# A vision tower whose patch convolution is split: two groups of images first, the other fourteen in strips between the first groups' chains

## Chip, cores, metric

The kernel runs on one NeuronCore of a Trainium2 chip. The metric is the device time of one execution in microseconds, lower is better, given as the median of several runs.

## What is computed

64 images of 2 x 104 x 104 are joined with four copies of themselves shifted by 4 pixels (zero filled), normalised per image over all ten channels, weighted, and turned into 13 x 13 tokens of 128 features by an 8 x 8 patch convolution. A class token is put ahead, and a graph layer, an attention layer and a gated mixture of eight experts follow.

```python
lu, ru, ld, rd = _shifts(x)
concat = jnp.concatenate((x, lu, ru, ld, rd), axis=1)
mean = jnp.mean(concat, axis=(1, 2, 3), keepdims=True)
var = jnp.var(concat, axis=(1, 2, 3), keepdims=True)
normed = (concat - mean) * jax.lax.rsqrt(var + EPS)
normed = normed * gamma[None] + beta[None]
y = jax.lax.conv_general_dilated(normed, W, window_strides=(PATCH, PATCH), padding='VALID', ...)
...
h = jnp.concatenate([broadcast cls_tok, h], axis=1)
h = h + gcn(_layernorm(h))                  # edges, relu, four 128x128 maps
hx = _layernorm(h); causal attention with l2-normalised q, k; y = o @ Wo
gate = softmax(y @ gate_W + gate_b)
out = h + sum over 8 experts of gate * (gelu(y @ W1 + b1) @ W2 + b2)
```

## The kernel before, in words

The order of the work is written out by hand for five engines that meet only at semaphores: SP (loads and most stores), POOL, ACT, PE and DVE. Within an engine everything runs in the order of the program, so whatever waits holds up all that is queued behind it. Features lie on the 128 partitions, tokens along the free dimension.

**Convolution.** Row `p` of 13 rows of cells has 13 cells x 64 images = 832 columns. For each of 5 shifts DVE multiplies the loaded cells by gamma (L1006) into one of two sets of five `xg` tiles, and PE multiplies the product by `conv_w` (L650, in `conv`), five shifts summed in PSUM; `conv_ps` alternates between two PSUM pairs, so that ACT can copy row `p-1` out (L451, `tokens_out`) while PE works on row `p`. The convolution runs on cells that are not normalised; beside it ACT squares each row of cells (L446), DVE adds up the squares (L991) and POOL adds up the cells (L373). `prepare(p)` puts small pieces between the rows: one-hot tables (L946) for the graph matrix, the products of gamma and beta with the weights (L615), the graph maps and the split of weights into f16 pairs (L966 to L980).

**Image statistics.** After row 13 DVE reduces the sums to one column per image (L1019 to L1027), PE averages over partitions (L659), and DVE and ACT make a scale and a shift for all 64 images in `img` (L1030 to L1039).

**The chain of a group.** Four images (680 tokens) form a group, 16 groups. `early` corrects the tokens of a group with `img` (fix0 to fix3, L1066 and L1069), takes the layer norm (mean, dev, sq, var, three Newton steps of a reciprocal root on DVE at L1052 to L1059, cast back over partitions by PE at L692, xn) and applies the graph (edges, relu0 to relu3 at L485). `graph` adds the four maps (L664), the residual h2 and the second norm; `queries_keys` makes q and k and their norms. Then `attention` and the experts (`ffn`, 32 slots: L869 in, L564/L569 gelu, L1213 low part, L886 out, L1225 weighing). In the loop of groups each step of `early(g + 2)`, `graph(g + 1)` and `queries_keys(g + 1)` has a slot inside `ffn(g)` (tables EARLY_SLOTS and others). Groups 0 and 1 have no experts of earlier groups around them: their chains run after the convolution, one step after the other, before the first attention.

**Weights.** w1 and w2 (4 MB) are loaded late in the convolution and right after it; POOL splits them into f16 high and low parts (L387, L389, 32 instructions) while the chains of groups 0 and 1 run, and PE waits for all of them before the first experts. POOL also issues the accumulating stores of the expert outputs.

## Time and profile before

| | us |
|---|---|
| median of 3 runs (1611.28 to 1613.82) | 1611.56 |
| the profiled execution, its own time | 1615.64 |
| span of the profile | 1613.8 |
| PE busy / DVE busy / ACT busy / POOL busy | 1495.1 / 1211.3 / 1099.5 / 227.3 |
| mean granted TensorE clock (1 is 2.4 GHz) | 0.963 |

The profile is one execution. Busy is the time in which an engine worked on an instruction, and the idle time before an instruction is put down to whatever released it. A PE that is busy at the lower clock does half as much. The page cuts the span into 40 slices of 40.3 us:

```profile
PE   5993589999999999999999999999999999999998
...
DVE  7994358787868778787878787887878787877665
...
POOL 5376101010110101010101101010101010110101
PEclk8995589999999999999999999999999999999979
```

### The profile page before, as it was taken

What the parts mean: (1) busy time and instruction counts of PE and PEld (TensorE: products, weight loads), DVE (VectorE), ACT (ScalarE), POOL (GpSimd) and SP (SyncE); (2) the same over time, 40 slices, a digit from 0 to 9 for tenths busy, and PEclk for the clock granted to TensorE, in tenths of its full rate; (3) what the DMA queues carried; (4) which work ended last, traced back from release to release, by engine and by line L of the source; (5) the groups of instructions that cost most, each with busy time, mean ns of one, the idle gap of its engine ahead of it and who ended that gap; (6) DMA issues with size and microseconds to landing.
All of it is one profiled execution on the core that took longest, in us unless ns stands there. A gap on an engine that the chain in (4) does not pass through costs nothing.

```text
span 1613.8 us, 31251 instructions
## 1 busy us (share of the span) xinstructions
PE 1495.1 (93%) x10837; PEld 1020.8 (63%) x10837; DVE 1211.3 (75%) x2510; ACT 1099.5 (68%) x1879; POOL 227.3 (14%) x213
## 2 busy tenths in 40 slices
PE   5993589999999999999999999999999999999998
PEld 3551356666666666666666666666666666667665
DVE  7994358787868778787878787887878787877665
ACT  2321157777777777777777777777777777777766
POOL 5376101010110101010101101010101010110101
PEclk8995589999999999999999999999999999999979
DMA  5312004243333333241423333233324242433323
GB/s 189 116 65 79 9 5 110 36 104 43 97 51 95 42 89 52 59 80 26 112 35 104 43 95 47 92 43 91 49 45 94 33 109 38 104 43 97 53 88 53
DMA packets 33714, 113.48 MB, mean 70 GB/s; under 512 B 5008, under 2 KB 5008, under 8 KB 31120
## 3 DMA queue, kind: packets, MB, share of 16 engines
q0 software_dynamic: 18432, 44.57, 20.5%
q1 hardware_dynamic: 14960, 67.71, 11.4%
q10 hardware_dynamic: 288, 0.77, 0.1%
q8 instruction: 18, 0.29, 0.1%
q14 instruction: 16, 0.13, 0.0%
HBM read 62.56 MB, written 50.48 MB: 70 GB/s over the span
## 4 chain that ended last, share of the span: by engine, by line
PE 59%; DVE 28%; issue 7%; ACT 4%; DVEq 1%; DMA 1%; POOL 0%; POOLq 0%; ACTq 0%
PE pair L886 20%; PE pair L869 17%; PE pair L664 7%; DVE area L1213 5%; PE pair L650 4%; DVE area L1135 3%; DVE root_t L1055 2%; PE pair L783 2%; DVE area L1142 2%; DVE area L1225 2%; PE pair L692 1%; PE pair L676 1%; PE pair L817 1%; PE pair L739 1%; PE pair L810 1%
## 5 line engine op out<-in xcount | busy, mean ns | idle before, releaser
L564 ACT ACTIVATE area<-pair,pack_b_sb 128x680 f32<-128x680 f32 x512 | 422.8, 828 | 220.4 <-PE pair L869 217.8
L1213 DVE TENSOR_TENSOR area<-area 128x680 f16<-128x680 f32 x512 | 441.1, 864 | 149.3 <-ACT area L569 143.8
L886 PE MATMUL pair<-area,ws 128*128 128x340 f16 x3072 | 529.8, 307 | 12.9 <-DVE area L1225 11.8
L869 PE MATMUL pair<-area,ws 128*128 128x340 f16 x3072 | 527.1, 308 | 0.0
L886 PEld LDWEIGHTS pair<-area,ws 128*128 128x128 f16 x3072 | 284.3, 98 | 168.8 <-DVE area L1225 44.1
L869 PEld LDWEIGHTS pair<-area,ws 128*128 128x128 f16 x3072 | 297.8, 98 | 143.7 <-issue 0.2
L569 ACT ACTIVATE area<-pair,pack_b_sb 128x680 f16<-128x680 f32 x384 | 316.4, 824 | 0.0
L401 POOL DMA_DIRECT2D tower_out<-area x128 | 109.7, 857 | 1266.8 <-DVE area L1225 1205.3
L1225 DVE SCALAR_TENSOR_TENSOR area<-pair,pack_b_sb,area 128x340 f32<-128x340 f32 x256 | 134.0, 565 | 28.9 <-PE pair L886 19.9
L528 ACT ACTIVATE area<-pair,nbias,root 85x85 f32<-85x85 f32 (+1 forms) x256 | 112.4, 464 | 22.4 <-DVE nbias L1123 22.4
L650 PE MATMUL pair<-area,pack_a_sb 128*128 128x512 f32 (+1 forms) x260 | 97.1, 533 | 18.4 <-DVE area L1006 18.4
L650 PEld LDWEIGHTS pair<-area,pack_a_sb 128*128 128x128 f32 x260 | 50.7, 198 | 62.5 <-issue 42.9
L664 PE MATMUL pair<-area,gcn_m 128*128 128x340 f32 x256 | 83.4, 461 | 0.0
L1120 DVE TENSOR_REDUCE mx<-pair 85x4 f32<-85x340 f32 x64 | 41.0, 680 | 55.8 <-PE pair L787 55.8
L1006 DVE TENSOR_TENSOR area<-area,pack_a_sb 128x832 f32<-128x832 f32 x65 | 75.1, 1218 | 7.7 <-DMA pack_a_sb<-pack_a 6.3
L1211 DVE CAST area<-area 128x680 f16<-128x680 f32 x128 | 65.6, 513 | 19.7 <-ACT area L564 14.4
L451 ACT ACTIVATE ht<-pair 128x832 f32<-128x832 f32 x13 | 22.5, 1730 | 75.9 <-PE pair L650 75.9
L485 ACT ACTIVATE area<-pair,pack_b_sb 128x680 f32<-128x680 f32 x64 | 59.2, 935 | 20.2 <-PE pair L664 19.7
L373 POOL TENSOR_TENSOR area<-area 128x896 f32<-128x896 f32 x13 | 57.0, 4383 | 39.0 <-DMA area<-cells 38.0
L664 PEld LDWEIGHTS pair<-area,gcn_m 128*128 128x128 f32 x256 | 47.4, 195 | 18.0 <-issue 1.4
L798 PE MATMUL pair<-ident,area 85*85 85x85 f32 x384 | 45.4, 256 | 13.4 <-DVE area L1135 13.4
L1135 DVE TENSOR_SCALAR area<-area,rs 85x85 f32<-85x85 f32 (+1 forms) x256 | 55.7, 278 | 2.3
(182 smaller groups left out, 1640.7 us busy)
## 6 DMA issues: line engine op xcount, KB each, us to landing
tower_out<-area POOLq DMA_DIRECT2D x128, 340.0 KB, 4.6
area<-gate_scratch SPq DMA_DIRECT2D x16, 1360.0 KB, 9.9
area<-gate_scratch SPq DMA_DIRECT2D x16, 1020.0 KB, 7.1
area<-cells SPq DMA_DIRECT2D x14, 448.0 KB, 3.7
tower_out<-ht SPq DMA_DIRECT2D x16, 340.0 KB, 2.3
area<-gate_scratch SPq DMA_DIRECT2D x16, 340.0 KB, 4.4
area<-cells SPq DMA_DIRECT2D x13, 416.0 KB, 4.3
area<-w SPq DMA_DIRECT2D x1, 2048.0 KB, 10.1
```

Of the source, the lines that this page charges most:

```text
L401: pool.dma_start(out[:, g * T:(g + 1) * T], tmp[e % 2], accum_op=ALU.add).then_inc(out_done, 16)
L528: nc.scalar.activation(probs[:, b * SCORE + o0:b * SCORE + o0 + w], score_ps_at(b)[:, h, c * QC:c * QC + w], ACT.Exp, bias=nbias[:, n:n + ...
L564: nc.scalar.activation(two(hid[slot % NHID]), halves(hid_ps[slot % 2]), ACT.Gelu_apprx_tanh, bias=col(COL_B1 + slot)).then_inc(hid_ready, 1)
L569: nc.scalar.activation(two(hh[slot % NPART]), halves(hid_ps[slot % 2]), ACT.Gelu_apprx_tanh, bias=col(COL_B1 + slot)).then_inc(hhi_act, 1)
L650: last = mm(flat(conv_ps(p))[:, a:b], conv_w[:, s * D:(s + 1) * D], xg[p % 2][s][:, a:b], start=(s == 0), stop=(s == SHIFTS - 1))
L664: last = mm(fr_ps[:, j, 0:TH], lhs, rhs[:, j, :], start=start, stop=stop)
L869: last = mm(hid_ps[slot % 2][:, j, 0:TH], lhs[:, w], rhs[:, j * TH:(j + 1) * TH], start=(i == 0), stop=(i == 2))
L886: last = mm(eo_ps[:, j, 0:TH], lhs[:, w], rhs[:, j * TH:(j + 1) * TH], start=(m % CH == 0 and i == 0), stop=(m % CH == CH - 1 and i == 2))
L1006: v.tensor_tensor(xg[p % 2][s].rearrange("p (j b) -> p j b", b=B), src[:, c0 * B:(c0 + NP) * B].rearrange("p (j b) -> p j b", b=B), gv, AL ...
L1135: last = v.tensor_scalar(p, p, rs[:, n:n + 1], None, ALU.mult)
L1213: v.tensor_tensor(hl[slot % NPART], hid[slot % NHID], hh[slot % NPART], ALU.subtract).then_inc(hlo_ready, 1)
L1225: v.scalar_tensor_tensor(tmp[e % 2][:, j * TH:(j + 1) * TH], eo_ps[:, j, 0:TH], b2_s[:, e:e + 1], gbc[:, e * T + j * TH:e * T + (j + 1) * ...
```

## The change

The images are cut in two parts. The 8 images of groups 0 and 1 (`BA`) are loaded whole (`first0`, `first1`), multiplied and convolved at once for the full 13 x 13 cells (`gammas_first`, `conv_first`), and get their own sums (16 accumulating activations on ACT, borders on DVE) and their own factors. The other 56 images (`BZ`) are convolved as before in 13 rows of 728 columns, now counted as 65 points (row x shift). `xg` is a ring of six single products. The four tables FIRST_0, GRAPH_0, QK_0 and FIRST_1 name, for each step of the chains of groups 0 and 1, the point behind which it stands, on PE, ACT and DVE alike; PE_PREP, DVE_PREP and ACT_PREP do so for the preparations. The first two groups take their first mean with f32 matmuls straight from the tokens, so POOL has no part in it. The factors of the 56 images are finished between attention(0) and the first experts (15 small DVE instructions, no square root on ACT). A row of the strips has one PSUM pair (`eo_ps`, 7 and 6 cells in its two halves); its two halves are copied out by two ACT instructions, and the next row waits for them. The weights come expert by expert through four buffers: POOL splits experts 0 to 3 after its sums, and 4 to 7 ahead of its stores of group 0; PE waits for each expert's split inside the experts, in every group. `part_h`, `part_l` and `k_wide` have moved to other addresses.

```diff
+FIRST_0 = {"tail": 4, "fix0": 5, "fix1": 5, "fix2": 6, "fix3": 6, "mean": 7, "dev": 9, "sq": 10, "var": 11, "root0": 13,
+           "root1": 13, "root2": 13, "cast": 14, "xn": 16, "xn_lo": 16, "edges": 18, "relu0": 19, "relu1": 19,
+           "relu2": 19, "relu3": 19}
+GRAPH_0 = {"plain": 22, 0: 22, 1: 23, 2: 23, 3: 24, "h2": 26, "mean2": 27, "dev2": 29, "sq2": 30, "var2": 31,
+           "roots2": 33, "cast": 34, "hx": 36, "hx_lo": 36}
+QK_0 = {"q": 38, "sums_q": 40, "k": 40, "sums_k": 42, "root0": 44, "root1": 44, "root2": 44, "wide": 45,
+        "cast": 46, "kn": 48}
...
+BA = 2 * NB
+BZ = B - BA
+CHUNKS = ((0, 4), (4, 7), (7, 10), (10, NP))
+CELLS = ((0, 7), (7, NP))
+XG = 6
+PE_PREP = {7: 2, 10: 3, 14: 4, 19: 5}
+DVE_PREP = {4: 1, 6: 2, 9: 3, 17: 5}
+ACT_PREP = {3: 3, 11: 4, 15: 5, 20: 6}
...
-R1, R0 = 4, 4
+R1, R0 = 4, 3
...
+        M1, M0 = NG1 * NG1 * BA, NP * NP * BA
+        all1, all0 = take(M1, ws), take(M0, ws)
+        ag = [take(M0, ws) for _ in range(2)]
+        edge_a = take(2 * 4 * NG1 * BA, ws)
+        junk = [take(NG1 * NG1, ws) for _ in range(BA)]
...
+        row0 = [take(N0) for _ in range(R0)]
+        xg = [take(N0) for _ in range(XG)]
...
+            def weights(e):
+                if e >= 2:
+                    sp.wait_ge(wlo_done, 2 * (e - 1))
+                for k, w in enumerate((w1, w2)):
+                    sp.dma_start(staged[e][k], w[:, e * FF:(e + 1) * FF]).then_inc(w_in[e], 16)
+
+            sp.dma_start(all0, first0).then_inc(all0_in, 16)
+            sp.dma_start(all1, first1).then_inc(all1_in, 16)
+            sp.dma_start(packs["pack_b"][:, :], pack_b).then_inc(pack_b_in, 16)
             load0(0)
...
-            tokens_lo(0)
-
-            for i in range(2 * E):
-                part, first = (i * FF // STAGE, i * FF % STAGE) if i < E else (2, (i - E) * FF)
-                pool.wait_ge(w_in[part], 16)
-                hi, lo = (w1h, w1l) if i < E else (w2h, w2l)
-                w, src = slice((i % E) * FF, (i % E + 1) * FF), staged[part][:, first:first + FF]
-                pool.tensor_copy(hi[:, w], src).then_inc(whi_done, 1)
-                pool.wait_ge(whi_done, i + 1)
-                pool.tensor_tensor(lo[:, w], src, hi[:, w], ALU.subtract).then_inc(wlo_done, 1)
-
-            tokens_lo(1)
+            def split(e):
+                pool.wait_ge(w_in[e], 32)
+                for k, (hi, lo) in enumerate(((w1h, w1l), (w2h, w2l))):
+                    w, src = slice(e * FF, (e + 1) * FF), staged[e][k]
+                    pool.tensor_copy(hi[:, w], src).then_inc(whi_done, 1)
+                    pool.wait_ge(whi_done, 2 * e + k + 1)
+                    pool.tensor_tensor(lo[:, w], src, hi[:, w], ALU.subtract).then_inc(wlo_done, 1)
+
+            pool.wait_ge(part_step[0], 3)
+            pool.wait_ge(conv_a, len(CHUNKS))
+            for e in range(4):
+                split(e)
...
+                    if g == 0 and e + 4 < E:
+                        split(e + 4)
...
+            def sums_first():
+
+                act.wait_ge(all1_in, 16)
+                for n, func in enumerate((ACT.Copy, ACT.Square)):
+                    for b in range(BA):
+                        if n:
+                            act.wait_ge(sums_a, b + 1)
+                        nc.scalar.activation(junk[b], all1.rearrange("p (c b) -> p b c", b=BA)[:, b, :], func,
+                                             accum_out=stats[0][:, n * BA + b:n * BA + b + 1]).then_inc(sums_a, 1)
...
+            def tokens_out(p, j):
+                act.wait_ge(conv_done, 2 * p + j + 1)
+                t0, t1 = (1 + p * NP + c for c in CELLS[j])
+                dst = ht[:, BA * TOK:].rearrange("p (b t) -> p t b", t=TOK)[:, t0:t1, :]
+                nc.scalar.activation(dst, cells_ps(j).rearrange("p (j b) -> p j b", b=BZ), ACT.Copy).then_inc(tok_done, 1)
...
+            sums_first()
+            act.wait_ge(pack_b_in, 16)
+            nc.scalar.activation(ht[:, :].rearrange("p (b t) -> p t b", t=TOK)[:, 0, :],
+                                 col(COL_CLS).broadcast_to([128, B]), ACT.Copy).then_inc(tok_a, 1)
+            for c in range(len(CHUNKS)):
+                tokens_first(c)
+            squares(0)
+            prep_evac(2)
+            for n in range(POINTS):
+                p, shift = divmod(n, SHIFTS)
+                if shift == 0:
+                    squares(p + 1)
+                chain(n)
...
+            def conv_first():
+                for shift in range(SHIFTS):
+                    pe.wait_ge(mul_a, shift + 1)
+                    for c, (r0, r1) in enumerate(CHUNKS):
+                        last = mm(chunk_ps(c), conv_w[:, shift * D:(shift + 1) * D],
+                                  ag[shift % 2][:, r0 * NP * BA:r1 * NP * BA],
+                                  start=(shift == 0), stop=(shift == SHIFTS - 1))
+                        if shift == SHIFTS - 1:
+                            last.then_inc(conv_a, 1)
+                    if shift < SHIFTS - 1:
+                        last.then_inc(shift_a, 1)
+
+            def conv(n):
+                p, shift = divmod(n, SHIFTS)
+                pe.wait_ge(mul_done, n + 1)
+                for j, (c0, c1) in enumerate(CELLS):
+                    if shift == 0 and p == 0:
+                        pe.wait_ge(tok_a, 1 + 2)
+                    if shift == 0 and p:
+                        pe.wait_ge(tok_done, 2 * (p - 1) + j + 1)
+                    last = mm(cells_ps(j), conv_w[:, shift * D:(shift + 1) * D], xg[n % XG][:, c0 * BZ:c1 * BZ],
+                              start=(shift == 0), stop=(shift == SHIFTS - 1))
+                    if shift == SHIFTS - 1:
+                        last.then_inc(conv_done, 1)
+                if shift < SHIFTS - 1:
+                    last.then_inc(shift_done, 1)
...
+                if slot % CH == 0:
+                    pe.wait_ge(wlo_done, 2 * (slot // CH) + 1)
...
+            conv_first()
+            prepare(1)
+            for n in range(POINTS):
+                conv(n)
+                if n == 1:
+                    pe.wait_ge(tok_a, 1 + len(CHUNKS))
+                    image_stats(0, BA, fr_ps[:, 0, 0:2 * BA])
+                chain(n)
+                if n in PE_PREP:
+                    prepare(PE_PREP[n])
+            for n in LATE:
+                chain(n)
             attention(0, False, True)
-            pe.wait_ge(wlo_done, 2 * E)
+            pe.wait_ge(dev2_ready, 2)
+            image_stats(1, BZ, fr_ps[:, 1, 0:2 * BZ])
...
+            def gammas_first():
+                dve.wait_ge(pack_a_in, 16)
+                dve.wait_ge(all0_in, 16)
+                cells = all1.rearrange("p (i j b) -> p i j b", i=NG1, b=BA)
+                centre = all0.rearrange("p (i j b) -> p i j b", i=NP, b=BA)
+                for shift, (src, r, c) in enumerate(((centre, 0, 0), (cells, 1, 0), (cells, 1, 1), (cells, 0, 0), (cells, 0, 1))):
+                    if shift == 1:
+                        dve.wait_ge(all1_in, 16)
+                    if shift >= 2:
+                        dve.wait_ge(shift_a, shift - 1)
+                    gv = gam_v[:, shift].unsqueeze(3).broadcast_to([128, NP, NP, BA])
+                    v.tensor_tensor(ag[shift % 2].rearrange("p (i j b) -> p i j b", i=NP, b=BA),
+                                    src[:, r:r + NP, c:c + NP, :], gv, ALU.mult).then_inc(mul_a, 1)
...
+            def image_factors(part, n, b0, ps):
+
+                mean, var, root, half = (stats[part][:, (k + 2) * n:(k + 3) * n] for k in range(4))
+                scale, shift, step = img[:, b0:b0 + n], img[:, B + b0:B + b0 + n], img_step[part]
+                dve.wait_ge(part_ps[part], 1)
+                v.tensor_copy(mean, ps[:, 0:n]).then_inc(step, 1)
+                dve.wait_ge(step, 1)
...
+                for k in range(3):
+                    dve.wait_ge(step, 5 + 3 * k)
+                    v.scalar_tensor_tensor(half, root, -0.5, root, ALU.mult, ALU.mult).then_inc(step, 1)
+                    dve.wait_ge(step, 6 + 3 * k)
+                    v.tensor_tensor(half, half, var, ALU.mult).then_inc(step, 1)
+                    dve.wait_ge(step, 7 + 3 * k)
+                    v.scalar_tensor_tensor(scale if k == 2 else root, half, 1.5, root, ALU.add, ALU.mult).then_inc(step, 1)
...
+            prepare(0)
+            gammas_first()
+            sums_first()
+            for n in range(POINTS):
+                gammas(n)
+                if n % SHIFTS == SHIFTS - 1:
+                    square_sum(n // SHIFTS + 1)
+                chain(n)
+                if n in DVE_PREP:
+                    prepare(DVE_PREP[n])
+            for n in LATE:
+                chain(n)
+            sums_rest()
             attention(0, False, True)
+            dve.wait_ge(tok_done, 2 * NP)
+            image_factors(1, BZ, BA, fr_ps[:, 1, 0:2 * BZ])
```

Three places show the order. First PE, at the end of the convolution. Before (L650 is the convolution, L659 the statistics, L664 the mean, L676 the variance, L692 the cast of the roots of group 0), the last rows of the convolution and the first of the chain:

```order
L650 MATMUL pair<-area,pack_a_sb 128x512 [waits mul_done]
L650 MATMUL pair<-area,pack_a_sb 128x320
L659 MATMUL pair<-stat,count_m 128x128 [waits stat_step]
L664 MATMUL pair<-pack_a_sb,mean 128x340 [waits tokl_ready,split_step,tok_done]
L664 MATMUL pair<-pack_a_sb,mean 128x340 x3
L676 MATMUL pair<-mean_m,area 85x1 [waits sq_ready]
L676 MATMUL pair<-mean_m,area 85x1 x7
L692 MATMUL pair<-ident,root 128x85 [waits root_ready_ln1]
L692 MATMUL pair<-ident,root 128x85 x7
```

Now, at points 13 to 15 (L736 is the convolution, L777 the cast of the same group, L704 and L706 a preparation; the variance stands two points earlier):

```order
L736 MATMUL pair<-area,pack_a_sb 128x392 [waits mul_done]
L736 MATMUL pair<-area,pack_a_sb 128x336
L736 MATMUL pair<-area,pack_a_sb 128x392 [waits mul_done]
L736 MATMUL pair<-area,pack_a_sb 128x336
L777 MATMUL pair<-ident,root 128x85 [waits root_ready_ln1]
L777 MATMUL pair<-ident,root 128x85 x7
L704 MATMUL pair<-pack_b_sb,stage_sb 128x512 [waits act_prep]
L706 MATMUL pair<-pack_b_sb 128x1 x4
L736 MATMUL pair<-area,pack_a_sb 128x392 [waits tok_done,mul_done]
L736 MATMUL pair<-area,pack_a_sb 128x336 [waits tok_done]
```

The group's steps have convolution pieces between them, and a row's first pieces (the last two shown) wait for `tok_done`, the copy of the row before.

Second DVE, around the normalised tokens of group 0. Before (L1059 ends the roots, L1078 to L1083 make xn, L1088 is h2):

```order
L1059 SCALAR_TENSOR_TENSOR root<-root_t,root 85x8 [waits root_step_ln1]
L1078 TENSOR_TENSOR area<-area,pair 128x680 [waits root_cast_ln1]
L1080 CAST pack_a_sb<-area 128x680 [waits xn_ready]
L1083 TENSOR_TENSOR pack_a_sb<-area,pack_a_sb 128x680 [waits xnh_ready]
L1088 SCALAR_TENSOR_TENSOR ht<-pair,gcn_c,ht 128x680 [waits gcn_ps]
```

Now, at points 16 to 18 (L1244 ends the same xn, L1203 is a product of the convolution, L1079 to L1092 the fifth preparation):

```order
L1244 TENSOR_TENSOR area<-area 128x680 [waits xnh_ready]
L1203 TENSOR_TENSOR area<-area,pack_a_sb 128x728 [waits shift_done]
L1079 TENSOR_SCALAR gcn_m<-pair,pack_b_sb 128x128 [waits pe_prep]
L1079 TENSOR_SCALAR gcn_m<-pair,pack_b_sb 128x128 x3
L1082 SCALAR_TENSOR_TENSOR gcn_m<-pair,pack_b_sb,gcn_m 128x128 [waits dve_prep] x12
L1086 CAST wqk_h<-pack_b_sb 128x256
L1088 TENSOR_TENSOR wqk_l<-pack_b_sb,wqk_h 128x256 [waits split_step]
...
L1090 TENSOR_SCALAR gq<-pack_b_sb 128x1
L1092 TENSOR_TENSOR gq<-gq,pack_b_sb 128x1 [waits dve_prep]
L1203 TENSOR_TENSOR area<-area,pack_a_sb 128x728 [waits shift_done] x2
```

The 12 multiply-adds of the graph maps and the splits stand between the products of points 17 and 18, right behind xn. Before, they stood between two full rows.

Third DVE, from the gates of group 0 to its first expert. Before:

```order
L1189 RECIPROCAL gm<-gm 85x8 [waits gate_step]
L1191 TENSOR_TENSOR gts<-lge,gm 85x8x8 [waits gate_step]
L1211 CAST area<-area 128x680 [waits hid_ready]
L1213 TENSOR_TENSOR area<-area 128x680 [waits hhi_dve]
L1200 COPY gt_t<-pair 64x85 [waits gt_ps]
```

Now (L1352 the gates, L1372 and L1374 the first expert's high and low part):

```order
L1350 RECIPROCAL gm<-gm 85x8 [waits gate_step]
L1352 TENSOR_TENSOR gts<-lge,gm 85x8x8 [waits gate_step]
L1166 COPY statz<-pair 128x56 [waits part_psz,tok_done]
L1168 TENSOR_TENSOR statz<-statz 128x56 [waits img_stepz]
L1170 TENSOR_TENSOR statz<-pair,statz 128x56 [waits img_stepz]
...
L1182 SCALAR_TENSOR_TENSOR img<-statz 128x56 [waits img_stepz]
L1184 SCALAR_TENSOR_TENSOR img<-statz,img 128x56 [waits img_stepz]
L1372 CAST area<-area 128x680 [waits hid_ready,img_stepz]
L1374 TENSOR_TENSOR area<-area 128x680 [waits hhi_dve]
```

The 15 instructions of the factors of 56 images (L1166 to L1184) have come between the gates and the first expert.

## Rows read from the trace of the kernel before

**Rows 1.** Windows of the first 302 us, with busy time of each engine (columns first).

```profile
core 0: us, PE busy (x) PEld busy (x) DVE busy (x) ACT busy (x) POOL busy (x), PEclk, DMA share, GB/s
7.50:16.40 8.90, 8.76 (x20) 4.44 (x20) 8.90 (x6) 3.57 (x5) 7.59 (x4) 1.00 1.03 410
25.40:34.80 9.40, 9.40 (x19) 4.80 (x20) 9.40 (x11) 0.00 (x0) 2.28 (x1) 0.70 0.28 94
34.80:120.80 86.00, 84.20 (x270) 47.32 (x268) 79.85 (x93) 29.33 (x30) 47.91 (x10) 1.00 0.29 95
120.80:208.00 87.20, 35.71 (x167) 25.11 (x167) 36.60 (x86) 14.55 (x21) 31.08 (x34) 0.55 0.10 41
234.00:302.00 68.00, 67.18 (x513) 46.26 (x511) 54.25 (x111) 53.17 (x74) 7.66 (x8) 1.00 0.40 83
```

**Rows 2.** Chain of waits from 120.8 to 208 us, its summary by line.

```profile
by line: PE pair L664 20.3%; PE pair L676 8.5%; DVE stat L1019 7.4%; DVE root_t L1055 6.7%; PE pair L692 6.5%; PE pair L739 5.6%; ACT area L485 3.8%; DVE root_t L1057 3.7%; issue 3.4%; DVE root L1059 2.5%; DVE pack_a_sb L1083 2.3%; DVE area
```

**Rows 3.** Timeline of ACT, two evacuations of conv rows: start, us, engine, line.

```profile
84.23 1.74 ACT L451 ACTIVATE ht<-pair 128x832 f32<-128x832 f32 x1 [4.50 <-PE pair L650]
91.21 1.74 ACT L451 ACTIVATE ht<-pair 128x832 f32<-128x832 f32 x1 [4.49 <-PE pair L650]
```

**Rows 4.** Timeline of DVE: products and sums of one row; preparation; fixes; roots.

```profile
17.54 6.87 DVE L946 TENSOR_SCALAR stage_sb<-stage_sb,edge_f 128x128 f16<-128x128 f32 x16
62.08 1.11 DVE L966 TENSOR_SCALAR gcn_m<-pair,pack_b_sb 128x128 f32<-128x128 f32 x4
...
68.74 0.16 DVE L980 TENSOR_TENSOR gq<-gq,pack_b_sb 128x1 f32<-128x1 f32 x1
85.86 4.76 DVE L1006 TENSOR_TENSOR area<-area,pack_a_sb 128x832 f32<-128x832 f32 x5
90.54 1.08 DVE L991 TENSOR_TENSOR area<-area 128x896 f32<-128x896 f32 x1
119.21 1.68 DVE L1019 TENSOR_REDUCE stat<-area 128x64 f32<-128x896 f32 x1
...
130.09 0.40 DVE L1066 SCALAR_TENSOR_TENSOR area<-conv_u,img,conv_b 128x169 f32<-128x169 f32 x1
...
132.72 0.39 DVE L1069 SCALAR_TENSOR_TENSOR ht<-ht,img,area 128x169 f32<-128x169 f32 x1
...
202.21 0.17 DVE L1052 TENSOR_SCALAR root<-root_in 85x8 int32<-85x8 int32 x1 [3.64 <-ACT root_in L470]
...
203.98 0.16 DVE L1059 SCALAR_TENSOR_TENSOR root<-root_t,root 85x8 f32<-85x8 f32 x1
```

**Rows 5.** Timeline of ACT, the four relus of group 0.

```profile
153.32 3.34 ACT L485 ACTIVATE area<-pair,pack_b_sb 128x680 f32<-128x680 f32 x4 [11.91 <-PE pair L664]
```

**Rows 6.** Timelines of POOL and DVE where their instructions meet.

```profile
32.52 5.20 POOL L373 TENSOR_TENSOR area<-area 128x896 f32<-128x896 f32 x1 [10.55 <-DMA area<-cells]
38.50 2.08 POOL L373 TENSOR_TENSOR area<-area 128x896 f32<-128x896 f32 x1 [0.78 <-DMA area<-cells]
...
77.36 30.37 POOL L373 TENSOR_TENSOR area<-area 128x896 f32<-128x896 f32 x4 [10.72 <-DMA area<-cells]
98.27 13.16 DVE L1006 TENSOR_TENSOR area<-area,pack_a_sb 128x832 f32<-128x832 f32 x5 [0.97 <-PE pair L650]
```

**Rows 7.** Timeline of PE: first scores and first expert matmuls of groups 0 and 1.

```profile
213.93 1.12 PE L783 MATMUL pair<-area 64*85 64x85 f32 x16 [1.64 <-ACT area L518]
...
233.89 1.90 PE L869 MATMUL pair<-area,ws 128*128 128x340 f16 x12
...
302.75 1.12 PE L783 MATMUL pair<-area 64*85 64x85 f32 x16
...
321.03 1.89 PE L869 MATMUL pair<-area,ws 128*128 128x340 f16 x12
```

**Rows 8.** Timeline of POOL: first and last of the 32 weight splits.

```profile
135.41 0.61 POOL L387 CAST ws<-stage_sb 128x512 f16<-128x512 f32 x1
...
163.73 1.15 POOL L389 TENSOR_TENSOR ws<-area,ws 128x512 f16<-128x512 f32 x1
```

322 lines of the change are left out of this document (180 added, 142 removed).

## The prediction

> **What bounds the kernel now.** I read the page first: PE is busy 93% of the span, but the slices of the first 240 us fall out of the pattern, and the granted clock falls with them. Windows of that stretch come next [rows 1]. There are three regimes. From 34.8 to 120.8 us the convolution runs: PE is busy 84.2 of 86.0 us at the full clock, DVE 79.9. From 120.8 to 208 us the chains of groups 0 and 1 run: PE is busy 35.7 of 87.2 us at a mean clock of 0.55, DVE 36.6, ACT 14.6. Then attention(0) and, from 234 us, the experts, with PE busy 67.2 of 68.0 us. So the middle window is the place where time can be had. The chain of waits in it goes from PE to DVE to ACT and back, and no line has over 20.3% [rows 2]: it is bound by the sequence of steps, not by an engine. The change puts convolution work into these gaps, so I add up what PE must do at the full clock, and then what it must still wait for.
>
> **PE's work up to attention(0).** ACT copies the rows out 6.98 us apart [rows 3], which is a row of 832 columns at the full clock. The first eight images have 1352 columns per shift: 6.98 x 1352/832 = 11.3 us. A strip has 728: 6.11 us, 13 of them 79.4 us. The total is what it was. The preparations are the rest of the busy convolution window: 84.2 - 11 x 6.98 = 7.4 us [rows 1]. The chains are 35.7 x 0.55 = 19.6 us at the full clock, plus 0.9 us for the last edges, which lie behind 208 us (six f16 matmuls of 340 columns at 2.4 GHz). Two means are now f32: a column of the convolution takes four cycles (6.98 us for 4160 columns), so each mean is 8 passes of 340 columns where 4 stood, 1.1 us for both. Together 21.6 us. Sum: 11.3 + 79.4 + 7.4 + 21.6 = 119.7 us.
>
> **The start.** DVE makes the one-hot tables first now (6.9 us [rows 4]), from about 4 us because the small edge list is loaded first, and then a product of 1352 columns (0.95 us per 832 columns [rows 4], so 1.55 us). PE begins at 12.9 us instead of 7.5 us. Its first row took 8.8 us instead of 6.98 [rows 1], the clock still low: 1.8 us again.
>
> **What PE waits for.** I walk the tables point by point. PE needs 1.22 us per point, DVE 0.83 us for the product (4.76/5 x 728/832) and 0.95 us per row for the squares [rows 4]; DVE may be six products ahead. A chain step costs its DVE time, and DVE's lead is lost wherever it waits for PE.
> - Points 5 to 7: the factors of 8 images are 15 dependent small instructions at about 0.2 us (ten like them of the roots took 202.2 to 204.1 us [rows 4]), 3.1 us, then four fixes (130.1 to 133.1 us: 3.0 us [rows 4]), between products that PE needs at once. The square root that ACT has to do first comes on top. PE waits 4.7 us.
> - Points 11 to 14, sq and roots: 1.1 us.
> - Point 18: the fifth preparation took DVE from 62.1 to 68.8 us [rows 4]; 0.5 us of it has moved. It stands behind xn (2.3 us), when DVE has no lead left. 6.3 + 0.8 us for the next product, against 1.7 us that PE still has: it waits 5.4 us. Between the first two windows of [rows 1] PE had stood still for 9 us, and then the clock was low: a row took over 9.4 us for 6.98. I charge 3.3 us.
> - Point 20: four relus (3.35 us [rows 5]) stand before ACT's copy of row 3: 1.4 us.
> - Points 31 to 37, roots2 and hx: 1.9 us. Points 44 to 50, the roots of q and k and the fixes of group 1: 3.9 us. Points 56 to 60: 1.2 us.
> - Ends of rows. Before, two PSUM pairs alternated; now PE waits for the copy of the first half. The copy of 832 columns takes 1.74 us [rows 3], of 392 about 0.95 us, and PE's other half covers 0.56 us: 0.65 us with what the second half adds. At four row ends nothing else of PE's or DVE's covers it: 2.6 us.
>
> That is 25.5 us. Handoffs that I rounded away get 2 us.
>
> **POOL against DVE.** A sum of POOL takes 2.08 us alone and 5.20 us against DVE; four of them took 30.4 us while DVE's rows ran back to back, and seven of DVE's instructions then took 13.2 us instead of 7 [rows 6]. So each of the two holds up the other for whole instructions. The price for the change lies between 0 and 16 sums of 1.8 us (2.08 x 784/896), 29 us. DVE's work in the stretch is about 127 us, so it has leads in some two thirds of the points, which hide a delay of 1.8 us. I take 4 us, near the lower end. The Trainium skill, "SBUF — State Buffer", section "SBUF: two separate sides", calls the shared port pair an exclusive lock that the first comer holds for the whole instruction; by that rule, and this trace agrees with 2.9 us for products that take 1.0 us, the loss would be that of the first rival below if every sum met a product in need.
>
> Last piece of convolution: 12.9 + 1.8 + 119.7 + 25.5 + 2 + 4 = **165.9 us**.
>
> **From there to the experts.** ACT copies the last two halves (1.9 us) and two values tiles (0.8 us): first scores at 168.6 us, against 213.9 us before [rows 7]. That is -45.3 us. DVE reduces the sums of the strips just before (four at 1.68 x 784/896 = 1.5 us [rows 4], with the small ones 7.7 us); PE's tail covers all but 2 us of it: +2.0. From first scores to first expert attention(0) took 19.96 us at a partly low clock, attention(1) 18.28 us [rows 7]: -1.7, since PE is warm now. The factors of 56 images stand between the gates and the first expert on DVE, 15 dependent instructions at 0.23 us, and nothing covers them: +3.4. The weight splits went from 135.4 to 164.9 us [rows 8], beside idle engines. Now half of them, 14.7 us, fall into the experts of group 0, where DVE is busy 54.3 of 68.0 us [rows 1]. If none were absorbed this would cost 14.7 us, if DVE's 13.7 us of slack took them nothing; POOL acts only after an expert is weighed and is needed several slots later, so I take +2.0. The loads of these weights go behind the gates' broadcasts on SP and are in time for the same reason. PE's extra waits inside the experts are for a count reached long ago: 0, see the third rival. Moved tiles: 0.
>
> Sum: -45.3 + 2.0 - 1.7 + 3.4 + 2.0 = -39.6 us. From the profiled execution's 1615.6 us this gives 1576.0 us, and from the median, 4.1 us lower, **1572.0 us**.
>
> **Rivals.**
> 1. *The lock decides.* DVE, with 127 us of work and 29 us of POOL in its way, has no lead anywhere, and the walk gets 25 us longer: 1597 us. For it: two of the DVE rows above stretched just so. Against: DVE often waits for PE now, and POOL gets through then. A half-way case (12 us more) gives 1584 us. Chance 0.15.
> 2. *Fewer waits than I walked.* PE's queue and the ring of six hide half of the 25.5 us, and the clock does not fall at point 18: 1557 us. For it: PE lost almost nothing in the window from 34.8 us. Against: DVE's order is strict. Chance 0.14.
> 3. *Slower: the clock.* PE's gaps keep it at 1.2 GHz, as in the chain window, where it was busy 41% and the mean clock 0.55 [rows 1]. Each us of full-clock work then costs one more. It decides when 40 of the 119.7 us run low; if 60 us do, the result is 1632 us. Against: PE would be busy some 75% here, with one gap over 5 us. A cost for each of the 256 waits added to the experts would need 0.15 us each to eat the gain; PE's experts, with two waits a slot already, leave 0.8 us idle in 68 [rows 1]. Chance 0.04.
> 4. *No change:* the gain is given back in the experts of group 0, by late weights. It would need a stall of 39 us, and the last is needed some 50 us after the first experts start. Chance 0.01.
>
> **How the numbers follow.** The forecast, 0.66, has its own range of 1562 to 1583 us from the bounds of waits and lock. The faster rival reaches below it and the lock above; cutting both near their middles leaves 1558 to 1593 us. A measurement here tells 0.2%, 3.2 us, from no change. Faster by more than that: 0.95; within: 0.01; slower: 0.04.
>
> **What the profile would show.** Right: one stretch from about 13 to 166 us with PE some 75% busy at a clock near 1, no low-clock stretch at 120 to 208 us, first scores at 168 us, DVE with 15 small instructions just before its first expert cast, and a PE gap of 5 us around 62 us. Wrong: a clock near 0.5 for more than 20 us of it; products of 2.7 us in most rows (the lock); PE waiting for `tok_done` by more than 1 us per row; first experts' PE gaps of over 5 us in all; or a longer time per group from group 1 on.

## The result and the profile after

The changed kernel takes **1624.8 us** (median of 4 runs, 1623.4 to 1626.3) against 1611.6 us before: a ratio of 1.0078, 95% interval 1.0063 to 1.0093. It is slower by 13 us. The forecast was 1572.0 us, and the range of 1558 to 1593 us does not hold the time. The profiled execution took 1623.35 us; its forecast on the same footing was 1576.0 us, so 47 us are missing.

Most of the gain that was meant is there. The timeline of TensorE around the first experts of group 0, which answers to [rows 7]:

```profile
198.36 0.94 PE L944 MATMUL pair<-pack_b_sb,area 128*85 128x8 f32 x10
199.15 0.45 PE L745 MATMUL pair<-statz,count_m 128*128 128x112 f32 x2
199.44 1.90 PE L962 MATMUL pair<-area,ws 128*128 128x340 f16 x12
...
207.43 0.74 PE L981 MATMUL pair<-area,ws 128*128 128x340 f16 x4 [2.80 <-DVE area L1374]
```

The first experts start at 199.44 us, where they started at 233.89 us: 34.5 us sooner (45.0 had been forecast). So the rest of the kernel lost more than that. Windows of the stretch from the logits of group 1 to those of group 15, first of the kernel before, then of the changed one (columns as in [rows 1]):

```profile
319.69:1545.37 1225.68, 1188.43 (x9154) 824.42 (x9153) 945.49 (x2049) 921.94 (x1603) 114.96 (x125) 0.99 0.34 68
```

```profile
293.96:1553.58 1259.62, 1198.21 (x9154) 829.39 (x9153) 946.66 (x2049) 922.43 (x1603) 114.94 (x125) 0.99 0.33 67
```

The same 9154 matmuls, the same work of VectorE and ScalarE, and 33.9 us more. From the gate logits of one group to those of the next the groups took 87.7 to 87.9 us each before, and the last 84.3 us; now the first of these takes 87.78 us, the next twelve 90.5 to 90.9 us, and the last 84.4 us. The twelve are the turns of VectorE's loop that are entered by its jump back. The timeline of VectorE at the start of such a turn, before and after (the number in brackets is the idle time ahead, and what ended it; "issue" is a wait for nothing that the profile shows):

```profile
499.34 0.27 DVE L1191 TENSOR_TENSOR gts<-lge,gm 85x64 f32<-85x64 f32 x1
499.83 0.52 DVE L1211 CAST area<-area 128x680 f16<-128x680 f32 x1 [0.22 <-issue]
```

```profile
476.48 0.27 DVE L1352 TENSOR_TENSOR gts<-lge,gm 85x64 f32<-85x64 f32 x1
479.55 0.51 DVE L1372 CAST area<-area 128x680 f16<-128x680 f32 x1 [2.81 <-issue]
480.10 0.87 DVE L1374 TENSOR_TENSOR area<-area 128x680 f16<-128x680 f32 x1
```

TensorE, in the same turn, gets its half of the hidden units late:

```profile
481.22 1.39 PE L981 MATMUL pair<-area,ws 128*128 128x340 f16 x6 [2.40 <-DVE area L1374]
```

And the waits of VectorE from 290 to 1560 us name it as one item (us in total, times, longest):

```profile
DVE area L1372 <- issue: 33.7, 12, 3.0
```

Twelve waits, 33.7 us in sum: that is the whole loss of the loop. TensorE's busy time also grew, by 9.8 us, and the two windows' mean clock of 0.99 hides why: behind six of the twelve waits the granted clock fell to half for 3.4 us each. The one in this turn:

```profile
481.70:485.10 3.40, 3.40 (x18) 2.32 (x17) 3.07 (x13) 1.67 (x3) 0.00 (x0) 0.51 0.14 53
```

It cost next to nothing more: the six turns with such a stretch took 90.6 to 90.9 us, the six without 90.5 to 90.7. It came with the waits, and it is gone where they are gone (below).

Nothing in the loop's source had changed on VectorE. What had is where its code stands. The page's list of queues has a line for the fetches of instructions, before and after:

```profile
q14 instruction: 16, 0.13, 0.0%
```

```profile
q14 instruction: 78, 0.64, 0.1%
```

That is 62 packets of 8 KB more, and the trace has their times: the same five in each of the twelve turns (two turns have a sixth), in the turn above at 475.0, 477.6, 480.1, 490.7 and 523.8 us, the first three of them around the wait. The profile doesn't say which engine a packet of q14 is for; the pattern is tied to VectorE by its times. TensorE's queue (q8) has 18 and 19 packets, none of them between 310 and 1460 us. A count of the built programs gives VectorE 486 instructions ahead of its loop before and 538 after, and a loop body of 310 in both. (The first kernel's body must stay in the engine: from 380 to 1420 us q14 has two packets, at 606.4 and 776.7 us, and no pattern by turns.)

The Trainium skill, "Runtime: NRT & Kernel Launch", section "Instruction fetch mechanics", says that an engine other than TensorE holds 512 instructions, that fetching ahead is only sequential, and that a taken branch to a target outside what is held waits for the fetch. The trace agrees with the last: 2.8 us at the jump, and none before, with the same body of 310. The section's refill in blocks of 16 KiB, 256 instructions, does not fit: q14's packets are of 8 KB, and 128 instructions more ahead of the loop left it as bad as it was (below), where with blocks of 256 only 53 starts in a row could be bad for a body of 310.

### The profile page after: what moved, and what is told of

Read it like the earlier page. It is cut to its first block, busy times and chain, and to the rows that moved or that the text cites. A ratio compares the mean times of both kernels' runs of the same rounds, so it can differ in the third digit from the quotient of the medians.

```text
span 1621.6 us, 31694 instructions
## 1 busy us (share of the span) xinstructions
PE 1502.3 (93%) x10879; PEld 1027.2 (63%) x10879; DVE 1222.6 (75%) x2549; ACT 1104.0 (68%) x1925; POOL 207.5 (13%) x211
## 3 DMA queue, kind: packets, MB, share of 16 engines
q0 software_dynamic: 18432, 44.57, 20.4%
## 4 chain that ended last, share of the span: by engine, by line
PE 53%; DVE 20%; issue 7%; ACT 3%; DVEq 1%; DMA 1%; POOLq 0%; ACTq 0%
PE pair L981 21%; PE pair L962 17%; PE pair L749 5%; DVE area L1374 3%; DVE area L1296 3%; PE pair L874 2%; DVE root_t L1216 2%; DVE area L1303 2%; DVE area L1386 1%; PE pair L777 1%; PE pair L908 1%; PE pair L901 1%; PE pair L859 1%; DVE area L1372 1%; PE pair L830 1%
## 5 line engine op out<-in xcount | busy, mean ns | idle before, releaser
L1374 DVE TENSOR_TENSOR area<-area 128x680 f16<-128x680 f32 x512 | 442.6, 868 | 146.1 <-ACT area L618 140.5
L1386 DVE SCALAR_TENSOR_TENSOR area<-pair,pack_b_sb,area 128x340 f32<-128x340 f32 x256 | 134.0, 565 | 29.9 <-PE pair L981 17.3
L577 ACT ACTIVATE area<-pair,nbias,root 85x85 f32<-85x85 f32 (+1 forms) x256 | 112.4, 464 | 22.9 <-DVE nbias L1284 22.9
L736 PE MATMUL pair<-area,pack_a_sb 128*128 128x392 f32 (+1 forms) x260 | 95.2, 508 | 28.6 <-DVE area L1203 19.0
L1372 DVE CAST area<-area 128x680 f16<-128x680 f32 x128 | 66.8, 522 | 54.0 <-issue 33.7
L736 PEld LDWEIGHTS pair<-area,pack_a_sb 128*128 128x128 f32 x260 | 49.8, 203 | 65.5 <-DVE area L1203 36.4
L1203 DVE TENSOR_TENSOR area<-area,pack_a_sb 128x728 f32<-128x728 f32 x65 | 63.4, 1024 | 0.0
L514 ACT ACTIVATE ht<-pair 128x392 f32<-128x392 f32 (+1 forms) x26 | 19.8, 874 | 51.7 <-PE pair L736 51.7
L577 ACT ACTIVATION_READ_ACCUMULATOR area<-pair,nbias,root 85x1 f32 x256 | 54.3, 212 | 0.0
```

The costliest lines, as they stand in the source:

```text
L577: nc.scalar.activation(probs[:, b * SCORE + o0:b * SCORE + o0 + w], score_ps_at(b)[:, h, c * QC:c * QC + w], ACT.Exp, bias=nbias[:, n:n + ...
L736: last = mm(cells_ps(j), conv_w[:, shift * D:(shift + 1) * D], xg[n % XG][:, c0 * BZ:c1 * BZ], start=(shift == 0), stop=(shift == SHIFTS - 1))
L1372: v.tensor_copy(hh[slot % NPART], hid[slot % NHID]).then_inc(hhi_dve, 1)
L1374: v.tensor_tensor(hl[slot % NPART], hid[slot % NHID], hh[slot % NPART], ALU.subtract).then_inc(hlo_ready, 1)
L1386: v.scalar_tensor_tensor(tmp[e % 2][:, j * TH:(j + 1) * TH], eo_ps[:, j, 0:TH], b2_s[:, e:e + 1], gbc[:, e * T + j * TH:e * T + (j + 1) * ...
```

## The experiments

Two theories for the loop. **A:** the place of VectorE's loop body in its instruction stream decides. **B:** something that the change put into the loop does it, TensorE's 16 added waits per group or the moved tiles.

### Padding ahead of the loop

```
             for slot in range(SLOTS + LAG):
                 expert_slot(g, slot, later)
+                if not later:
+                    for k in range(slot * 55 // SLOTS, min(55, (slot + 1) * 55 // SLOTS)):
+                        v.memset(pad[:, k:k + 1], 0.0)
```

**55 memsets in the changed kernel.** Expected:

> The changed kernel with 55 memsets of one column each put on VectorE between the steps of group 0's experts, ahead of its loop; everything else as it is. Theory A (where VectorE's loop body of 310 instructions stands in its instruction stream decides whether it is fetched anew in every turn): the loop's turns go back from 90.6 to about 87.8 us, the wait of 2.8 us ahead of the first CAST of each turn goes to about 0.3, the fetches of 8 KB in the loop go away, and the time falls by 13 x 2.8 = 36, to about 1588. Theory B (TensorE's 16 added waits per group, or the moved tiles, make the turns longer): turns stay at 90.6 us and the time at 1625, since both are untouched. The memsets themselves: some 0.06 us each beside TensorE's work, nothing on the path.

Measured: 1589.5 us, ratio to before 0.9861 (0.9835 to 0.9888). The window of the same fourteen groups, and the page's lines on fetches and on the first cast:

```profile
291.80:1517.58 1225.78, 1188.50 (x9154) 824.75 (x9153) 945.57 (x2049) 920.83 (x1603) 114.62 (x125) 0.99 0.32 68
```

```profile
q14 instruction: 18, 0.15, 0.0%
...
L1373 DVE CAST area<-area 128x680 f16<-128x680 f32 x128 | 67.3, 526 | 20.4 <-ACT area L614 15.2
```

1225.78 us is the kernel before to 0.1 us, with TensorE's added waits and the moved tiles still in it. The fetches by turns are gone, the half-clock stretches too (none from 210.0 us to 1503.7 us), and the cast's idle time fell to 20.4 us (it was 19.7 before the change, 54.0 after). 55 instructions that do nothing made the kernel 35 us faster.

**52 memsets in the kernel before.** The `memset` edit is the same with 52. Expected:

> The kernel before with 52 such memsets in the same place, so that its VectorE loop starts at the same instruction count as that of the changed kernel (both have 535 instructions ahead of it). Theory A: turns of 87.8 become 90.6 us, about 1611.6 + 36 = 1648. Theory B: nothing changes, 1611.6.

Measured: 1648.8 us, ratio 1.0222 (1.0198 to 1.0246). The loss appears in a kernel that has nothing else of the change. Its list of VectorE's groups shows the same item (busy, mean ns, then idle before):

```profile
L1212 DVE CAST area<-area 128x680 f16<-128x680 f32 x128 | 65.7, 514 | 54.1 <-issue 34.4 <-ACT area L565 16.8
```

**128 memsets in the changed kernel.** Expected:

> The changed kernel with 128 such memsets in place of 55. Theory A in the form that the phase against blocks of 128 instructions (8 KB of 64 bytes) decides: the phase is that of the unpadded one, so turns of 90.6 us and about 1625. If more instructions ahead of the loop were good by themselves (a longer distance, not the phase): 1588 as with 55. Theory B: 1625 too, so this run tells apart the two forms of A and not A from B.

Measured: 1624.4 us, ratio 1.0064 (1.0042 to 1.0086), turns of 90.5 to 90.7 us (the first of the twelve 92.0, with the clock at half for 6.8 us in it), and

```profile
q14 instruction: 79, 0.65, 0.1%
```

So distance does not help, the phase does: with 128 more instructions than the changed kernel the loss is the same.

**20 memsets in the changed kernel** (one execution). Expected:

> The changed kernel with 20 memsets. By blocks of 128 instructions a body of 310 lies in three blocks if it starts at 0 to 74 in a block and in four from 75 to 127. The count ahead of the loop as built is 538 plus what the runtime puts ahead (unknown, 49 to 100 by the runs before and after): with 20 the start is still in the bad part if that is under 82, and in the good part from 82. So turns are either 90.6 us (time 1625) or 87.8 us (time 1589), and nothing between; a mean of the two would speak against blocks.

Measured: 1622.0 us, turns of 90.5 to 90.8 us, 78 packets in q14. The bad side again, and nothing between. (In this trace the wait stands as "issue" in seven turns, and in five it is put down to ScalarE, with the same turns of 90.5 us and more.)

(The expectations count thirteen turns; twelve is right, since the first is entered without a jump. The 535 in one of them leaves out three instructions at the start of the program: 538.)

Theory A is shown, B is out: the loss was taken away and put back by instructions that do nothing, in both kernels. Counts ahead of the loop, less the multiples of 128: 102 and 81 are good, 26 (three times) and 46 are bad. A body of 310 instructions covers three blocks of 128 or four, as it lies, and good starts covering three and bad ones four fits every run (with 49 to 81 instructions of the runtime's ahead of the program). That three blocks stay in the engine and four don't is a reading that fits; no run showed what the engine holds.

### Group 0's experts

The rest of the shortfall is 1589.5 - 1572 = 17 us. The next edits all stand on the kernel with 55 memsets. The first: the factors of the 56 images three instructions at a time, and GpSimd's store ahead of its splits.

```
-            image_factors(1, BZ, BA, fr_ps[:, 1, 0:2 * BZ])
-            dve.wait_ge(img_step[1], 15)
...
+                    if not later and slot < 5:
+                        image_factors(1, BZ, BA, fr_ps[:, 1, 0:2 * BZ], 3 * slot, 3 * slot + 3)
...
-                    if g == 0 and e + 4 < E:
-                        split(e + 4)
                     pool.dma_start(out[:, g * T:(g + 1) * T], tmp[e % 2], accum_op=ALU.add).then_inc(out_done, 16)
+                    if g == 0 and e + 4 < E:
+                        split(e + 4)
```

> As the first of these, and two edits in group 0's experts: the 15 dependent instructions for the factors of the 56 images stand three at a time behind VectorE's steps 0 to 4 instead of all ahead of step 0, and GpSimd's store of expert e is issued ahead of the splits of expert e+4 instead of behind. If the gaps of TensorE of 2.8 us at 204.6 and of 2.2 + 0.9 us behind the late stores come from these, group 0's experts go from 96.4 to between 87.5 and 91, and the time is 5 to 9 us under the first of these (about 1581). Rival: what was hidden comes up behind (VectorE's steps themselves, the loads of the weights): less than 3 us under it.

Measured: 1591.7 us (0.9874, 0.9852 to 0.9896), and group 0 takes 96.1 us from logits to logits against 95.6. The rival holds. The gap of 2.8 us is gone, and in its place TensorE waits 1.47 us at 206.7, 1.11 at 213.8, 0.98 at 215.8 and 2.58 at 237.3, each for VectorE.

The store alone, with the factors left in one block:

> Only the second of the two edits of the run with both: GpSimd's store of expert e ahead of the splits of e+4. The factors stay in one block. If the gaps of TensorE behind the late stores (1.1, 1.1 and 2.1 us in the run with 55 memsets) come from the order on GpSimd, they go, group 0's experts take 91 to 93 us in place of 95.6, and the time is near 1586. Rival (VectorE is the full engine of this stretch, and the stores were only named last): group 0's experts stay within 1 us of 95.6 and the gaps are put down to VectorE's own steps.

Measured: 1589.8 us (0.9857, 0.9837 to 0.9878), group 0 in 96.1 us. The rival again: the late store was the wait that ended last, and not the cause. What both edits left as it was is VectorE's load. In this stretch of 94.4 us of the kernel with the spread preparation (below) VectorE is busy 77.5 us, and 71.6 us of 91.65 when no split of GpSimd lies in it (the last experiment):

```profile
190.70:285.10 94.40, 87.45 (x662) 60.20 (x660) 77.53 (x219) 66.27 (x115) 25.42 (x25) 0.98 0.36 87
```

```profile
196.50:288.15 91.65, 87.13 (x662) 60.23 (x660) 71.56 (x219) 66.21 (x115) 8.45 (x9) 0.98 0.31 66
```

The same 219 instructions take VectorE 6.0 us more beside GpSimd's 17 us of splits.

### The end of the convolution

```
             pool.wait_ge(conv_a, len(CHUNKS))
+            pool.wait_ge(stat_step, 8)
             for e in range(4):
                 split(e)
```

> All of this call stand on the changed kernel with 55 memsets ahead of VectorE's loop (1589.5). Here GpSimd begins the splits of experts 0 to 3 only when VectorE's sums of the 56 images are through (about 180 us) in place of 144.8 us. If the splits held VectorE up in the last 20 us of the convolution: the roots at 151.6 take 2 us in place of 6, TensorE's gap of 3.4 at 158.5 goes to about 1, and the last piece of the convolution ends 3 to 5 us sooner (near 170 in place of 174); the splits then meet attention of group 0 and may take 1 to 3 us of it back. Time 1585 to 1588. Rival (the roots were stretched by something else): the gap stays and the time is that of the first, 1589.

Measured: 1586.7 us (0.9844, 0.9827 to 0.9862). The last piece of the convolution ends at 166.8 us, where it ended at 175.9 us with the 55 memsets alone. Of these 9.1 us, 2.0 were there before any split ran: the same strip starts at 141.7 us here and at 143.7 us there, and the splits begin there at 146.3 us. Executions of the same code differ by as much (the changed kernel and those with 55, 128 and 20 memsets, the same up to there, end the convolution at 174.4 to 176.5 us); here the kernel with 55 memsets alone had the clock at half for 3.4 us from 80.6 us on, and this one did not. The splits' part is 7.1 us, still more than was expected. VectorE's timeline at the roots of group 1, in the changed kernel with the splits beside it, and in this one:

```profile
152.24 0.16 DVE L1216 SCALAR_TENSOR_TENSOR root_t<-root 85x8 f32<-85x8 f32 x1
152.43 1.01 DVE L1218 TENSOR_TENSOR root_t<-root_t,root_in 85x8 f32<-85x8 f32 x1
153.47 0.52 DVE L1220 SCALAR_TENSOR_TENSOR root<-root_t,root 85x8 f32<-85x8 f32 x1
```

```profile
149.58 0.16 DVE L1218 SCALAR_TENSOR_TENSOR root_t<-root 85x8 f32<-85x8 f32 x1
149.78 0.16 DVE L1220 TENSOR_TENSOR root_t<-root_t,root_in 85x8 f32<-85x8 f32 x1
149.97 0.16 DVE L1222 SCALAR_TENSOR_TENSOR root<-root_t,root 85x8 f32<-85x8 f32 x1
```

An instruction on eight columns takes 1.01 us instead of 0.16 when it meets a split. Windows from that strip to the end of the convolution, of the kernel with 55 memsets alone and of this one:

```profile
143.74:175.94 32.20, 25.30 (x90) 15.21 (x89) 30.03 (x33) 8.90 (x13) 23.48 (x18) 0.84 0.13 44
```

```profile
141.73:166.84 25.11, 22.28 (x90) 13.74 (x89) 21.84 (x33) 8.90 (x13) 2.63 (x2) 0.93 0.00 1
```

The work is the same, 90 matmuls and 33 instructions of VectorE. VectorE is busy 8.2 us less for it. TensorE's gaps fall from 6.9 to 2.8 us, and its busy time from 25.3 to 22.3 us as the mean clock rises from 0.84 to 0.93. But attention of group 0 pays for it: from first scores to first experts 25.9 us against 20.2 us. Its two windows, alone and with the splits:

```profile
177.70:197.90 20.20, 17.64 (x141) 12.43 (x142) 16.37 (x44) 12.77 (x42) 0.00 (x0) 1.00 0.00 1
```

```profile
168.60:194.50 25.90, 19.83 (x140) 13.78 (x141) 22.89 (x44) 12.91 (x42) 14.01 (x16) 0.87 0.16 55
```

VectorE's same 44 instructions take 22.9 us instead of 16.4. Of the 7.1 us, 5.7 are given back at once. Group 0's experts stay at 95.6 us.

### VectorE's preparation

```
-DVE_PREP = {4: 1, 6: 2, 9: 3, 17: 5}
+DVE_PREP = {4: 1, 6: 2, 9: 3, 17: 5, 18: 6, 19: 7, 20: 8, 21: 9}
...
-                if p == 5:
+                if p in (5, 6, 7, 8):
...
-                    for k in range(4):
+                    for k in (p - 5,):
...
+                if p == 9:
```

> VectorE's fifth preparation (16 instructions on gcn_m, six splits and two on gq, 6 us together) stands in five pieces behind points 17 to 21 in place of all behind point 17. If TensorE's gap of 5.3 us at 66.7 is this block ahead of the product of point 18: the gap falls to 1 to 3 us, spread over points 18 to 22, and everything behind comes 3 to 4 us sooner: 1586. Rival: VectorE is as full as TensorE there, and the same microseconds come up in pieces; the time stays at 1589.

Measured: **1581.7 us**, ratio 0.9812 (0.9795 to 0.9829), 8 us under the kernel with the memsets alone, twice what was expected. The gap of 5.32 us at point 18 is 0.37 us in its place:

```profile
71.81 1.67 PE L737 MATMUL pair<-area,pack_a_sb 128*128 128x392 f32 x2 [5.32 <-DVE area L1204]
```

```profile
68.30 1.49 PE L737 MATMUL pair<-area,pack_a_sb 128*128 128x392 f32 x4 [0.37 <-DVE area L1206]
```

TensorE's gaps from 60 to 90 us fall from 8.2 to 3.8 us, and the mean clock from 60 to 80 us rises from 0.83 to 0.91. The last piece of the convolution ends at 170.4 us, 5.6 us sooner; some 1.7 us of this may be the half clock from 80.6 us on again, which three of the seven executions with the undivided block have. VectorE had slack behind the block, and not in it (with one block it stood idle for 4.2 us ahead of 81.8 us).

The three edits together, late splits, store first and spread preparation:

> The three edits of this call together. If each is worth what its theory gives and none takes back another's: 1589.5 - 3 - 4 - 3 = about 1580. If VectorE is the full engine from 160 us on, what the late splits and the stores give comes back in the experts of group 0: 1584 to 1587.

Measured: 1582.9 us (0.9808, 0.9785 to 0.9832). The convolution ends at 165.3 us, but attention takes 29.6 us and group 0 96.2 us. The time lies between the two that were expected (1580, and 1584 to 1587). Beyond the spread preparation nothing is left of the others.

### Where else the splits could go

Apart, behind the sums of rows 9 and 12, one at the old place, one after VectorE's sums:

```
+                if a in (9, 12):
+                    pool.wait_ge(part_step[0], 3)
+                    pool.wait_ge(conv_a, len(CHUNKS))
+                    split((a - 9) // 3)
             pool.tensor_tensor(rim_x, rim_x, row1[NP % R1], ALU.add).then_inc(xsum_done, 1)
+            split(2)
+            pool.wait_ge(stat_step, 8)
+            split(3)
```

> On the kernel with 55 memsets and VectorE's preparation in five pieces (1581.7). GpSimd's splits of experts 0 to 3 are taken apart: expert 0 behind the sum of row 9 (about 101 us), expert 1 behind that of row 12 (about 128), expert 2 where all four began, expert 3 only after VectorE's sums of the 56 images. If a split costs VectorE what the two share and costs TensorE only where VectorE has no lead, the gap of 3.3 us at 154 and the slow end of the convolution go (last piece about 163 in place of 170.4), and attention of group 0 stays near 20 to 22 us in place of the 26 that it took with all four splits in it: first experts at about 186 in place of 192.3, time near 1576. Rival: VectorE has no lead anywhere from 90 us on; the splits then open gaps at 101 to 107 and 128 to 133 of the size that goes at 154, and the time stays within 2 us of 1581.7.

Measured: 1586.3 us (0.9838, 0.9813 to 0.9863; its runs scatter from 1579.4 to 1591.0). The new gaps came, 2.09 us at 103.6 and 1.88 us at 128.5, and attention took 22.6 us. The profiled execution has its first experts at 190.5 us, 1.8 sooner than with the splits in one piece. No gain that these runs can tell: it is neither clearly the theory's 1576 nor below 1581.7.

With it, the square root of the degrees one point later (`ACT_PREP = {4: 3, ...`):

> As the run before, and ScalarE's square root of the degrees behind the evacuation of point 4 in place of behind point 3, so that the row's evacuation doesn't wait for VectorE's degree sum. TensorE's gap of 3.5 us at 39.6 should fall to 0.5 to 1, all behind it comes 3 us sooner: about 1573. Rival: VectorE's second preparation, which waits for this root, comes later and takes the gap over (a gap of 2 to 3 us at 42 to 46): time as the run before.

Measured: 1582.0 us (0.9802, 0.9772 to 0.9832), not to be told from the others. The gap was not taken away: it is 3.24 us at 39.6, and ended by VectorE's product instead of ScalarE's evacuation. So the time is the rival's, and the place is not (it had the gap at 42 to 46 us). It looks as if several waits ended together there; this wasn't tested further.

Last, all eight experts' splits ahead of group 0's experts (the loop over `E` in place of 4, and the loads of experts 4 to 7 ahead of the stores):

> On the kernel with 55 memsets and the preparation in five pieces (1581.7, group 0's experts 94.4 us). All eight experts' weights are loaded and split ahead of group 0's experts (GpSimd from about 141 us on), none between its stores. If the splits of experts 4 to 7 (about 18 us of GpSimd between 220 and 260) slow VectorE and with it the experts of group 0: these take 90 to 91 us (the 87.1 of before and the 2.8 of the factors) in place of 94.4. The four splits more then lie in attention of group 0, which takes 2 to 6 us longer, as it did with the four of the run with the late splits: time 1580 to 1584. Rival (what slows group 0's experts is the factors, the clock after their gap and the late store alone): they stay at 93 to 95, and the time rises to 1584 to 1588.

Measured: 1584.0 us (0.9824, 0.9806 to 0.9843). Group 0's experts take 91.7 us from logits to logits, and attention 25.8 us, with a gap of 5.49 us in it:

```profile
185.14 1.16 PE L885 MATMUL pair<-ident,area 85*85 85x85 f32 x6 [5.49 <-DVE area L1294]
```

This is close to the theory on both sides (90 to 91 us, and 2 to 6 us more in attention), and the time stands on the border between theory and rival. Four experts' splits cost some 3 us in the experts, some 6 us in attention and 7 us at the end of the convolution; no place that was tried is free.

## Why the prediction was wrong

**The step that failed** is "PE's extra waits inside the experts are for a count reached long ago: 0 [...] Moved tiles: 0", which closed the account of everything behind group 0. The two zeros are right in themselves: with 55 memsets, the waits and the moved tiles in place, fourteen groups take 1225.78 us against 1225.68. What had no term was the instructions that the change adds ahead of VectorE's loop, 52 of them. They shift the loop's body, and each jump back then waits 2.8 us: 12 x 2.8 = 33.7 us, of the 47 that are missing. The text had the sign to look for, "a longer time per group from group 1 on", with no mechanism and no price; the rival that ends slower was the clock, which stayed at 0.94 in the stretch of the convolution. With this one cost taken away by padding, the rest of the forecast stands inside its range, at 1589.5 us.

The other terms, each against the profile after:

- *Start:* 12.9 + 1.8 us forecast; TensorE begins at 10.5 us, and its first 24 matmuls take 1.5 us more than the next ones at their pace.
- *Gaps of TensorE up to the last piece:* of the 25.5 us 3.3 are a charge for the clock, so 22.2 + 2 + 4 = 28.2 us were forecast. The gaps behind the start sum to 29.9 us. Right in sum. At point 18, 5.4 us were forecast and 5.32 came; the relus took 2.5 us instead of 1.4. Points 5 to 7 came as 3.5 us ahead of 39.6, ended by ScalarE.
- *The clock:* 3.3 us were charged. It was at half for 20.4 us in four stretches, in which TensorE was busy 15.8 us: 7.9 us.
- *TensorE's work:* 119.7 us forecast. Of 134.0 us busy, 124.6 are left when the 7.9 of the clock and the 1.5 of the start are taken off: 4.9 us more. The price per point was right (strings of one, two and three points take 1.39, 2.61 and 3.83 us, so 1.22 us each), but each string has 0.17 us beyond it, and where a gap follows nothing covers this. By an estimate, 22 gaps x 0.17 = 3.7 us. No run tested it, and the ends of matmuls are modelled in the profile.
- These four put the last piece at 174.4 us in place of 165.9: -2.7 + 1.7 + 4.6 + 4.9 = 8.5 us.
- *GpSimd against VectorE:* the 4 us were reckoned for GpSimd's sums alone. (The reading beside them was off: the row of 13.2 us is five products, 2.9 us each where they take 1.0 alone, and not seven instructions in place of 7 us.) The splits of experts 0 to 3 were not placed: they lie from 144.8 to 166.3 us, in the last strips of the convolution, and moving them away takes 7.1 us off these strips, 4.1 of gaps and 3.0 of busy time. So most of the clock's excess came with the splits: a stretched VectorE makes gaps, and the half-clock stretches lie behind them (in the changed kernel from 150.6 and from 157.5 us on). That the convolution then ends 0.9 us from the forecast is in part luck: in that execution start and gaps are some 5 us under their forecasts, and work and clock some 6 us over.
- *Attention of group 0:* 18.3 + 2.0 us forecast, 23.3 us measured. In that execution the clock was at half for 6.8 us, from 191.6 us on. The kernels with 128, 55 and 20 memsets, whose code is the same up to there, had 3.4, 0 and 0 us of it and took 21.8, 20.2 and 20.2 us. So the forecast was right where the clock held, and the 3.0 us are the luck of one execution; why it fell there the traces don't say.
- *Group 0's experts:* 87.1 + 3.4 + 2.0 = 92.5 us forecast, 96.4 measured. The factors make a gap of 2.8 us (3.4 forecast), and the splits cost some 3 us where 2.0 were forecast: 94.4 us with them and 91.7 without, in the kernels with the spread preparation.

In sum 7.6 us up to the first scores, 3.0 in attention, 3.9 in group 0's experts, 33.7 in the loop: 48 us, for 47 missing.

The rivals: the lock (1597 us) was right in kind and in order of size, 7 us at the convolution's end and 3 in the experts, but as GpSimd's splits and not as its sums. Of TensorE's other signs, the convolution stretch was busy 82% (134.0 of 163.9 us) at 0.94, and no stretch at half clock was longer than 6.8 us.

Padded, the change is worth what it was meant for in part: 1589.5 us, inside the forecast's range. With the preparation spread over five points it is 1581.7 us, 1.9% under the kernel before (0.9812, 0.9795 to 0.9829).

## What to carry to other kernels

When an edit adds or removes instructions ahead of a long loop, count them per engine, and look at three places in the profile after: the number of packets in each instruction queue, a wait ahead of the first instruction of each turn (mostly put down to "issue"), and the time per turn. If it grew with no change in the loop, pad the code ahead by some tens of instructions in a place with slack and run it again before judging the edit; here that moved the verdict from 0.8% slower to 1.4% faster. And a block of small work on an engine with no lead can cost nearly its whole length, even if the same engine idles 10 us later: cut it in pieces. That is no rule for every stretch: in group 0's experts the same cut turned one gap into four and gave nothing.

## What the runs showed of the hardware that was not expected

- VectorE's loop of 310 instructions is fetched anew in every turn or in none, as its start lies: 16 to 18 packets on queue q14 in a whole execution against 77 to 79, five of 8 KB in each turn, and 2.8 us at each jump. Adding 128 instructions of padding changes nothing; adding 55 does.
- TensorE's loop is over twice as long (661 instructions in its body before, 677 after) and its queue had 18 and 19 packets, none between 310 and 1460 us: not fetched anew.
- An instruction of VectorE on 8 columns takes 0.16 us alone and up to 1.01 us beside GpSimd's splits of 512 columns, whose own take 0.60 to 1.7 us and once 4.32 us. Sixteen such splits (14.0 us of GpSimd) added 6.5 us to VectorE's 16.4 us in attention.
- A wait of TensorE of some 2.4 us can be followed by a stretch of 3.4 us at half the clock, and need not be: it was behind six of the loop's twelve waits.
